# The setup stage of a three-pass decoder kernel: angles counted in turns, work spread over engines, weights loaded ahead

## The reference

```python
dt = jnp.exp(log_dt)                     # per channel (256)
A, C = A_re + 1j * A_im, C_re + 1j * C_im    # 256 channels x 64 states
dtA = dt[:, None] * A
dC = C * (jnp.exp(dtA) - 1.0) / A
powers = jnp.exp(dtA[:, :, None] * jnp.arange(L))     # L = 128 positions
K = 2.0 * jnp.einsum('dn,dnl->dl', dC, powers).real   # the convolution's taps
...
V = x_vision @ Wv
scale_in, shift_in = jnp.split(c_t @ W_film_in + b_film_in, 2, axis=-1)
x = x * (1.0 + mod_gate * scale_in) + mod_gate * shift_in
y = s4d(x, log_dt, A_re, A_im, C_re, C_im, D_skip)    # convolution with K, plus D_skip * x
```

## Time and profile before

| | |
|---|---|
| median of 3 runs | 7270.23 us (7249.97 to 7282.78) |
| profiled execution | 7281.31 us, its span 7279.5 us |
| TensorE busy | 6712.2 us, 92% |
| VectorE busy | 5405.5 us, 74% |
| GpSimd busy | 4589.0 us, 63% |
| ScalarE busy | 4456.3 us, 61% |
| setup, to the end of its barrier | 132.9 us |

### The profile page before, as it was taken

One profiled execution on the slowest core, in us unless ns is written; L12 is line 12 of the kernel. 1 busy time (PEld: TensorE's weight loads), 2 busy tenths in 40 slices (PEclk: granted clock), 3 DMA queues, 4 the chain that ended last, 5 costly groups with the idle time before them and its releaser, 6 DMA issues. The chain is left out here.

```text
span 7279.5 us, 106079 instructions
## 1 busy us (share of the span) xinstructions
PE 6712.2 (92%) x24272; PEld 3702.6 (51%) x24272; DVE 5405.5 (74%) x13962; ACT 4456.3 (61%) x9788; POOL 4589.0 (63%) x3991
## 2 busy tenths in 40 slices
PE   2899999999999999999999999997789999999997
PEld 1354444544445444454445544454656666666664
DVE  5588888888888888888888888887436666666665
ACT  2778888788877888878888788885212112221111
POOL 0788888888888888888888888897011112111111
PEclk6999999999999999999999999998889999999998
DMA  1666556665666666666556655566611111111110
GB/s 42 137 142 151 140 144 156 154 146 144 143 150 153 147 144 143 152 153 149 143 135 151 158 147 144 137 151 176 208 35 33 32 32 32 32 32 32 32 32 20
DMA packets 554199, 834.94 MB, mean 115 GB/s; under 512 B 169180, under 2 KB 207389, under 8 KB 551713
## 3 DMA queue, kind: packets, MB, share of 16 engines
q1 hardware_dynamic: 552768, 820.23, 46.1%
q10 hardware_dynamic: 864, 8.65, 0.3%
HBM read 745.91 MB, written 74.45 MB: 113 GB/s over the span
## 5 line engine op out<-in xcount | busy, mean ns | idle before, releaser
L1250 POOL TENSOR_TENSOR arena<-arena 128x512 f32<-128x512 f32 x2048 | 2581.9, 1276 | 276.4 <-DVE arena L1175 249.2
L875 PE MATMUL psum<-arena 128*128 128x512 f32 x4096 | 2192.3, 632 | 43.7 <-POOL arena L1250 37.9
L1175 DVE TENSOR_TENSOR_SCAN arena<-arena,psum 128x512 f32<-128x512 f32 x1024 | 1237.2, 1208 | 385.4 <-ACT arena L1044 297.9
L1263 POOL TENSOR_TENSOR arena<-arena 128x512 f32<-128x512 f32 x1024 | 1331.6, 1300 | 149.8 <-PE psum L875 149.5
L1031 ACT ACTIVATE arena<-arena 128x128 f32<-128x128 f32 x4096 | 1304.8, 396 | 134.0 <-PE psum L860 133.6
L1179 DVE TENSOR_TENSOR_SCAN arena<-psum,arena 128x512 f32<-128x512 f32 x1024 | 1234.8, 1206 | 87.4 <-ACT psum L1044 26.0
L875 PEld LDWEIGHTS psum<-arena 128*128 128x128 f32 x4096 | 712.0, 199 | 599.0 <-issue 385.4
L1044 ACT ACTIVATE arena<-arena 128x508 f32<-128x508 f32 x1024 | 738.5, 721 | 57.8 <-DVE arena L1175 57.1
L1829 POOL TENSOR_SCALAR arena<-arena 128x4 f32<-128x4 f32 x160 | 37.0, 231 | 1164.9 <-DVE arena L1690 1164.9
L860 PEld LDWEIGHTS psum<-arena 128*128 128x128 f32 x4096 | 518.7, 146 | 489.2 <-issue 441.4
L1044 ACT ACTIVATE psum<-arena 128x508 f32<-128x508 f32 x1024 | 701.5, 685 | 64.8 <-DVE arena L1179 31.0
(11 more groups left out here) (218 smaller groups left out, 10103.8 us busy)
## 6 DMA issues: line engine op xcount, KB each, us to landing
arena<-bc_scratch SPq DMA_DIRECT2D x1152, 512.0 KB, 5.3
arena<-in_xT_dram SPq DMA_DIRECT2D x32, 512.0 KB
arena<-in_x_dram SPq DMA_DIRECT2D x32, 512.0 KB, 7.8
x_scratch<-arena SPq DMA_DIRECT2D x32, 512.0 KB, 5.7
xin_scratch<-arena SPq DMA_DIRECT2D x128, 128.0 KB, 2.5
arena<-kernel_scratch SPq DMA_DIRECT2D x32, 512.0 KB, 7.0
arena<-x_scratch SPq DMA_DIRECT2D x32, 512.0 KB, 3.8
out_dram<-arena SPq DMA_DIRECT2D x32, 512.0 KB
```

What stands on the lines that cost most here:

```text
L875: pe.matmul(y_ps, ident, ring[:, u % RING], start=False, stop=n == NS - 1).then_inc(S["nsum"], 1)
L1175: dve.tensor_tensor_scan(s, decay_sb[:, u // 2 % 2], bx_ps[:, u // 2 % 2], 0.0, ALU.mult, ALU.add)\
L1250: pool.tensor_tensor(h, h, Cb[:, u // 2 % PAIRS, u % 2], ALU.mult).then_inc(S["hc"], 1)
L1263: pool.tensor_tensor(ring[:, u % RING], uu[par][:, c], Bb[:, state(u)], ALU.mult)\
```

## The change

It rewrites `setup` and takes the loads out of the head of `pass1`.

- Angles: b is scaled to turns (1/2pi) when it is made. Each row is one tensor_scalar (times a constant, plus a phase that for 32 of the rows is a per-partition pointer); the row is rounded and the rounded value subtracted once; ScalarE's sine takes a scale of 2 pi. This is done in three blocks of rows: the coefficient's 3, the 16 low ones, the 16 high ones, each with its own sine.
- VectorE's helper `tt` issues scalar_tensor_tensor (times 1.0) where it issued tensor_tensor.
- GpSimd does the film fold and multiplies the low powers by their magnitudes in eight products of 512 columns.
- The high powers' products are done in two halves of 128 channels, 1024 columns each; TensorE takes the first four groups of channels after the first half.
- Loads: SP issues log_dt and s4 first, on a semaphore of their own, then the skip weight, xT and eight of pass 1's weights; ScalarE's queue issues the film loads. The folded film is loaded back once it is stored.
- Tap stores: sixteen of half the length, eight behind the fourth skip and eight behind the eighth, and setup doesn't wait for them. SP waits for them at the end of pass 1, ahead of the Toeplitz loads, ScalarE ahead of the first write to one of the two buffers they leave from.
- The buffers of pass 1's weights, of xT, of one z and of yg move so that setup can fill them.

The diff, cut to its core:

```diff
         @block.sync
+            for dst, src in ((dt, i_["log_dt"]...), (s4[0:SM], i_["s4"]), (s4[SM:P], i_["s4"])):
+                sp.dma_start(dst, src).then_inc(s4_ld, 16)
+            sp.wait_ge(dsk_zero, 1)
+            sp.dma_start(dsk[NG - 1:NG], i_["d_skip"]).then_inc(skip_ld, 16)
+            sp.dma_start(sh.xT, i_["xT"][:, :, 0:T]).then_inc(sh.xT_ld, 16)
             for dst, src in (
-                (wv, i_["wv"]), (wf, i_["wf"]), (brow, i_["film_b"]),
-                (gate, ...), (s4[0:SM], i_["s4"]), (s4[SM:P], i_["s4"]), (dt, i_["log_dt"]...), (gb, ...),
+                (sh.win, i_["in_proj"]), (sh.wxp, i_["x_proj"]), (sh.vec1, i_["vec"]), (sh.wdt, i_["dt_proj"]),
+                (sh.wout, i_["out_proj"]), (sh.wq, i_["wq"]), (sh.wk0, i_["wk"][0:P]), (sh.wk1, i_["wk"][P:CTX]),
             ):
-                sp.dma_start(dst, src).then_inc(loaded, 16)
+                sp.dma_start(dst, src).then_inc(sh.w1_ld, 16)
...
-            sp.wait_ge(skipped, 8)
-            for k in range(NG):
-                sp.dma_start(kr_d[:, 16 * k:16 * k + 16][None], ksbuf[k:k + 1]...).then_inc(kst, 16)
-            sp.wait_ge(film_st, 48)
-            sp.wait_ge(kst, 16 * (NG + 1))
+            sp.wait_ge(film_st, 64)
+            sp.dma_start(sh.wf0, wf_d[0:P, 0:2 * D]).then_inc(sh.w1_ld, 16)
+            sp.dma_start(sh.wf1, wf_d[P:CTX + 1, 0:2 * D]).then_inc(sh.w1_ld, 16)
+            for h in range(2):
+                sp.wait_ge(skipped, 4 * (h + 1))
+                for k in range(NG):
+                    sp.dma_start(kr_d[h * DQ:(h + 1) * DQ, 16 * k:16 * k + 16][None],
+                                 sh.taps[h][k:k + 1].rearrange("p (d j) -> p d j", j=16)).then_inc(sh.taps_st, 16)
         @block.gpsimd
+            pool.wait_ge(film_ld, 16 * 5)
+            pool.wait_ge(film_sb, 4)
+            pool.wait_ge(bias_row, 3)
+            for n, (rows, v) in enumerate(((P, fold0), (CT2, fold1), (1, brow))):
+                scale, shift = v[0:rows, 0:D], v[0:rows, D:2 * D]
+                pool.tensor_tensor(half_x[0:rows], scale, gb[0:rows, D:2 * D], ALU.mult).then_inc(gain_step, 1)
+                pool.wait_ge(gain_step, 2 * n + 1)
+                pool.tensor_tensor(shift, shift, half_x[0:rows], ALU.add).then_inc(gain_step, 1)
+                pool.wait_ge(gain_step, 2 * n + 2)
+                pool.tensor_tensor(scale, scale, gb[0:rows, 0:D], ALU.mult).then_inc(gained, 1)
+            pool.wait_ge(mags, NR)
+            pool.wait_ge(sines, 2)
+            for e in range(0, NR, 2):
+                pool.tensor_tensor(tab[:, e:e + 2], tab[:, e:e + 2], mag[:, e:e + 2], ALU.mult).then_inc(powers, 1)
         @block.tensor
-            pe.wait_ge(tables, 1)
+            pe.wait_ge(powers, NR // 2)
             for q in range(8):
+                pe.wait_ge(tables, q // 4 + 1)
         @block.scalar
+            for dst, src in ((wv, ...), (wf, ...), (brow, ...), (gate, ...), (gb, ...)):
+                act.dma_start(dst, src).then_inc(film_ld, 16)
...
-            act.wait_ge(angles, 1)
-            act.activation(tab, tab, ACT.Sin).then_inc(sines, 1)
+            for n, (lo, hi) in enumerate(((RE, NE), (0, NR), (NR, RE))):
+                act.wait_ge(angles, n + 1)
+                act.activation(tab[:, lo:hi], tab[:, lo:hi], ACT.Sin, scale=TWO_PI).then_inc(sines, 1)
         @block.vector
             def tt(o, x, y, op):
-                link(dve.tensor_tensor(o, x, y, op))
+                link(dve.scalar_tensor_tensor(out=o, in0=x, scalar=1.0, in1=y, op0=ALU.mult, op1=op))
...
+            for lo, hi in ((RE, NE), (0, NR), (NR, RE)):
+                for e in range(lo, hi):
+                    last = dve.tensor_scalar(tab[:, e], b, float(steps[e]), phase[e], ALU.mult, ALU.add)
+                link(last)
+                link(dve.tensor_scalar(turns[:, lo:hi], tab[:, lo:hi], MAGIC, -MAGIC, ALU.add, ALU.add))
+                whole, part = (v[:, lo:hi].rearrange("p e d -> p (e d)") for v in (turns, tab))
+                dve.scalar_tensor_tensor(out=part, in0=whole, scalar=-1.0, in1=part, op0=ALU.mult, op1=ALU.add)\
+                   .then_inc(angles, 1)
...
-            tt(tab[:, 0:NR + NG], tab[:, 0:NR + NG], mag, ALU.mult)
-            dve.memset(turns[:, 0, 0:1], 0.0).then_inc(tables, 1)
+            for h in range(2):
+                cols = slice(h * DQ, (h + 1) * DQ)
+                g0, g1 = tab[:, NR:NR + NG, cols], tab[:, NR + NG:RE, cols]
+                link(dve.tensor_tensor(g0, g0, er[:, None, cols].to_broadcast([P, NG, DQ]), ALU.mult))
+                link(dve.tensor_tensor(g1, g1, ei[:, None, cols].to_broadcast([P, NG, DQ]), ALU.mult))
+                link(dve.tensor_tensor(g0, g0, g1, ALU.add))
+                dve.tensor_tensor(g0, g0, mag[:, NR:NR + NG, cols], ALU.mult).then_inc(tables, 1)
```

More of the change, by code:

```diff
@@ L64 @@
 SCAN_COLS = 16896
+WEIGHT_COLS = SCAN_COLS + 4 * C * T
 KEPT = 2
@@ L281, in sem @@
             return sems.named(n)
[L282 removed]
+        s4_ld, film_ld, skip_ld = sem("s4_ld"), sem("film_ld"), sem("skip_ld")
+        film_mm, film_sb, film_st = sem("film_folded"), sem("film_gated"), sem("film_stored")
         consts, dve_step, dt_ready, mag_a = sem("s_consts"), sem("dve_step"), sem("dt_ready"), sem("mag_a")
[L284 to L285 removed]
+        angles, sines, mags, tables, kmm, ksb = (sem(n) for n in (
+            "angles", "sines", "mags", "tables", "kernel_mm", "kernel_sb"))
+        powers, gain_step = sem("powers"), sem("gain_step")
         zero_st, bias_row, tanh_a = sem("zeros_ready"), sem("bias_row"), sem("tanh_a")
@@ L406, in _ @@
+            dve.memset(ph[SM:P, 2:3], -2.0).then_inc(consts, 1)
             dve.memset(dsk, 0.0).then_inc(dsk_zero, 1)
-            dve.wait_ge(loaded, 16 * 9)
+            dve.wait_ge(s4_ld, 16 * 3)
             dve.wait_ge(dt_ready, 1)
             dve.tensor_tensor(a, are, dt, ALU.mult).then_inc(mag_a, 1)
[L410 to L414, removed]
@@ L415, in _ @@
-            link(last)
-            dve.wait_ge(consts, 10)
-            groups = ((0, NR + NG, ph[:, 2:3], ph[:, 0:1]), (NR + NG, NR + 2 * NG, ph[:, 3:4], ph[:, 1:2]),
-                      (NE - 3, NE - 2, 0.25, TWO_PI / 4), (NE - 2, NE, 0.0, 0.0))
-            for lo, hi, turn, _ in groups:
-                last = dve.tensor_scalar(turns[:, lo:hi], tab[:, lo:hi], 1 / TWO_PI, turn, ALU.mult, ALU.add)
-            link(last)
-            link(dve.tensor_scalar(turns, turns, MAGIC, -MAGIC, ALU.add, ALU.add))
@@ L423, in _ @@
-            for part in (C1, C2, C3):
-                flat = tab.rearrange("p e d -> p (e d)")
-                link(dve.scalar_tensor_tensor(out=flat, in0=turns.rearrange("p e d -> p (e d)"), scalar=-part,
-                                              in1=flat, op0=ALU.mult, op1=ALU.add))
-            for lo, hi, _, phase in groups:
-                last = dve.tensor_scalar(tab[:, lo:hi], tab[:, lo:hi], phase, PI, ALU.add, ALU.min)
-            link(last)
-            dve.tensor_scalar(tab, tab, -PI, None, ALU.max).then_inc(angles, 1)
@@ L432, in _ @@
-            t, em, den, er, ei, x, qr, qi = tmp
+            link(dve.scalar_tensor_tensor(out=b, in0=aim, scalar=1 / 6.283185307179586, in1=dt, op0=ALU.mult, op1=ALU.mult))
+            dve.wait_ge(consts, 6)
+            late = [16 * (NG - 1 - e) for e in range(NG)]
+            steps = [NR - 1 - e for e in range(NR)] + late + late + [1, 1, 0.5]
+            phase = [ph[:, 0:1]] * (NR + NG) + [ph[:, 1:2]] * NG + [0.25, 0.0, 0.0]
+            for lo, hi in ((RE, NE), (0, NR), (NR, RE)):
[6 more added lines that the diff above has]
+                   .then_inc(angles, 1)
```

132 lines of the change are left out of this document (61 added, 71 removed).

## The result

The changed kernel takes 7227.88 us (median of 5, 7214.3 to 7229.3) against 7269.1 (median of 5) of the kernel before in the same comparison: ratio 0.9946, 95% interval 0.9931 to 0.9961, so 28 to 50 us less. Its profiled execution has a span of 7227.1 us.

The account below looks back on a forecast made before the run. A chain of dependent VectorE work, not TensorE, was taken to set setup's end. Terms -3.0 - 31.9 - 3.7 - 8.8 + 12.2 - 8.2 - 8.8 = -52.2 us took the median from 7270.2 to 7218, range 7192 to 7238.

Parts of the forecast that it names:

- the likeliest case: Whole kernel: the forecast itself, 52.2 us gained, median 7218 and profiled span 7227; chance 0.50.
- 80 to 102: Sign at the end of setup: pass 1's first matmul, forecast at 93 us; outside these bounds the prediction is wrong.
- 1, loads: Start of setup: log_dt and s4 first on SP, film loads on ScalarE's queue; -3.0 us, bounds 0 and -4.5.
- 2, angles: VectorE's angle rows in setup, computed in turns with fewer passes: 23.9 us instead of 55.8, -31.9.
- 3, fold off VectorE: Film fold in setup leaves VectorE's chain: -3.7 us as a removal, its price on GpSimd counted separately.
- 4, products: Table products before the kernel matmuls: first half 5.0 us instead of 13.8, second half hidden; -8.8.
- 6, exclusion: Setup: GpSimd's time adds to VectorE's chain where VectorE works on SBUF alone; +12.2 us, bounds 0 and 16.
- Rival A: Setup: no mutual exclusion of GpSimd and VectorE, so no added time; -64.4 us, 7206; chance 0.20.
- B: Setup: VectorE always wins, GpSimd comes last and releases TensorE; -47.4 us, 7223; chance 0.12.
- 7, tap stores: End of setup: no wait for landing, -4.6 us, and eight half-length issues behind the last skip, -3.6; together -8.2.
- 8, entry: From setup's barrier to pass 1's first matmul: the wait for weights goes, 13.5 us becomes 4.7; -8.8.

## Why the prediction was right, and where it was not

The time, 7227.9, lies in the range and 10 above the forecast; the likeliest case was the right one in kind. Setup gave 44.0 and not 52.2: entry came at 101.0 against 93, only 1 us inside the 80 to 102 outside which the prediction would have called itself wrong. The forecast of the profiled span, 7227, was met by chance, since the other 8.4 us lay behind entry. Step by step:

- **1, loads: failed.** -3.0 forecast, +2.8 measured (11.05 to 13.81). I let s4 have half the wire and called landing behind all film loads the worst case; it landed at 13.3, beyond my bound of 10.5. (The arithmetic was loose too: 10.5 less 9.3 is 1.2, so half of the rate gives 6.8, not 7.5.) The runs show the price of the second queue instead: 12.9 with the film loads alone, 6.5 when SP issues everything. The rule of turns between queues, which I had named beside it (the Trainium skill, "DMA: Bandwidth & Descriptors", Queues, rings and completion order), I had read as half of the bytes, 7.5. It speaks of turns by packets, not of bytes, and in the trace, with small pieces against large ones the bytes went one to six at first; the short queue ended before the long one by only 0.8 us (12.9 against 13.6). This one step is 5.8 of the 8.2 us.
- **2, angles: right.** 31.9 forecast. From the first row to the instruction behind the angles it is 24.2 us in the run with nothing beside it (14.82 to 39.01), 31.6 less; the pointer shows as 0.268 us a row (4.29/16) against 0.205.
- **3, fold off VectorE: right,** 3.7.
- **4, products: right.** 67.42 to 72.57 is 5.15 us; 8.7 less, forecast 8.8; the second half was hidden.
- **6, exclusion: right in kind, too small.** 12.2 forecast, 13.9 measured. I let GpSimd use the reciprocals for 3.5 us. It never met them: back to back it was done at 43.9, before VectorE got there (in the run with one queue it met one, and there both did run at once). Without the reciprocals my own sum was 15.7; GpSimd's work lasted 16.8 (27.17 to 43.95) and cost 13.9, so two misses partly offset each other, and what hid the 2.9 was not taken apart. And the shape was other than I drew: not turn about with the small products, but a run of eight that VectorE waited out. Rival A is excluded, and B, that VectorE always wins, has the winner wrong: its time, near 70, would nearly have fitted, but VectorE's last product released the matmuls, not GpSimd. The rule of an exclusive lock for a whole instruction (the Trainium skill, "SBUF — State Buffer", Who interferes with whom) holds in the runs (the row with PSUM's operand is free, the same row with SBUF's isn't, and the rounding passes do exclude GpSimd, as the rule had it and no row before showed). The price here came from how turns were passed on: a run of eight products, not one.
- **7, tap stores: right sum, wrong reason.** 8.2 forecast, 8.0 measured (91.09 to 96.10 against 118.44 to 131.5). The 4.6 us of landing went, the issues went from 8.4 to 5.0; but the whole stores at the new place cost 5.8, so halving them gave 0.8 us of that, and the rest was not the pieces' number: the buffer's start accounts for 1.9 of issue in the kernel before, and the 0.8 left over is less than the 1.0 by which that kernel's issues differ from one execution to another.
- **8, entry: right,** 8.6 measured (96.10 to 101.00), 8.8 forecast; 9.5 when undone.

Together: +2.8 - 31.6 - 3.7 - 8.7 + 13.9 - 8.0 - 8.6 = -43.9, against 44.0 read from the entry.

## What to carry to other kernels

Before giving a part of VectorE's work to GpSimd, count both on SBUF as one resource: if VectorE's chain there has no holes, GpSimd's time is added to it, and GpSimd is the slower (8.1 us of VectorE's work became 13.9). Give work a later place beside TensorE first; here that took the fold to zero. Put what starts the chain alone at the head of one queue, and look at the byte at which a buffer starts when its pieces are small.

## What the runs showed of the hardware

- A VectorE tensor_scalar with its tensor in SBUF, or a product of two tensors there, that meets GpSimd products issued back to back waits for the whole run: 10.55 us for one row, 11.82 for a pass of 2.29, 12.64 for four products that take 1.81. If GpSimd waits between them, VectorE gets in at the gaps (longest 2.0).
- A reciprocal, one tensor in SBUF, ran beside GpSimd's products at 1.75 us as alone, and they at 0.72 and 0.63.
- The tensor_scalar with its operand in PSUM is not held (6.35 us for 16 with and without GpSimd), but runs at 0.40 us instead of 0.27.
- Nine loads of 2.13 MB: in by 10.4 to 11.2 us on one queue (five executions), by 13.6 on two (one execution), where the queue with 0.64 MB ended at 12.9 beside one with 1.48; of its bytes 0.13 MB had gone by 6 us, of the other's 0.72.
- 2048 pieces of 64 bytes read from SBUF: 8.43 to 9.43 us of issue and 5.8 to 6.3 to land with the buffer 24 bytes behind a 64-byte boundary (four executions), 6.56 and 4.2 on it (one).
